# Output stage of a gated cross-attention and memory kernel: the stores move from ScalarE's queue to GpSimd's

## The reference

```
x = x + tanh(g_xattn) * softmax(Q K^T / sqrt(2048)) ctx      Q from layernorm(x), K from ctx
h = layernorm(x)
x = x + tanh(g_ffn) * (h + gate * aux),   aux = top-8 of 512 slots, softmax, values, down (128) and up (2048)
```

## Time and profile before

| | |
|---|---|
| median of 3 runs | 1082.8 us (1082.01 to 1083.5) |
| the profiled execution | 1081.9 us, of which the span of its instructions is 1079.8 us |
| granted TensorE clock, mean | 0.986 |
| PE busy | 1040.5 us (96%) |
| DVE busy | 784.7 us (73%) |
| ACT busy | 561.7 us (52%) |
| POOL busy | 183.2 us (17%) |
| output stage | from about 913 us to the end of the span |
| DMA | 218.93 MB over the span, mean 203 GB/s |

### The profile page before, as it was taken

The page is one execution under the profiler, slowest core; times in us unless marked ns, Lnnn a source line. Parts: engine busy times, 40 slices in busy tenths (PEclk is TensorE's granted clock), DMA queues, the critical chain, the costliest instruction groups (busy, mean ns, idle before and its releaser), DMA issues. The chain is left out here.

```text
span 1079.8 us, 19306 instructions
## 1 busy us (share of the span) xinstructions
PE 1040.5 (96%) x6778; PEld 995.8 (92%) x6778; DVE 784.7 (73%) x1845; ACT 561.7 (52%) x881; POOL 183.2 (17%) x351
## 2 busy tenths in 40 slices
PE   6999999998989999999999999999999994999997
PEld 6999999998989999999999999999999993888885
DVE  4889645466668787777777687877778766788785
ACT  3644777546435545454545445454545444555643
POOL 0007001000002222223231222222232321000000
PEclk9999999999999999999999999999999996999999
DMA  8556658598269965743445735257434418999999
GB/s 237 158 157 197 265 185 329 195 309 274 71 186 246 232 154 137 192 119 114 113 120 147 182 81 152 78 134 195 119 114 113 120 39 265 376 391 407 406 422 380
DMA packets 109615, 218.93 MB, mean 203 GB/s; under 512 B 48388, under 2 KB 64804, under 8 KB 95528
## 3 DMA queue, kind: packets, MB, share of 16 engines
q1 hardware_dynamic: 99784, 180.68, 55.0%
q10 hardware_dynamic: 9216, 33.56, 8.0%
q0 software_dynamic: 576, 4.19, 0.9%
HBM read 174.10 MB, written 54.79 MB: 212 GB/s over the span
## 5 line engine op out<-in xcount | busy, mean ns | idle before, releaser
L56 PE MATMUL tk_bank<-b_weights,k_turned 128*128 128x384 f32 (+2 forms) x1088 | 359.8, 331 | 3.4 <-DVE k_turned L1428 1.6
L58 PE MATMUL tk_bank<-b_weights,k_turned 128*128 128x384 f32 (+2 forms) x1088 | 350.9, 322 | 0.0
L57 PE MATMUL tk_bank<-b_weights,k_turned 128*128 128x384 f32 (+2 forms) x1088 | 350.7, 322 | 0.0
L56 PEld LDWEIGHTS tk_bank<-b_weights,k_turned 128*128 128x128 f32 x1088 | 205.2, 189 | 6.8 <-issue 2.6
L57 PEld LDWEIGHTS tk_bank<-b_weights,k_turned 128*128 128x128 f32 x1088 | 205.4, 189 | 1.2
L58 PEld LDWEIGHTS tk_bank<-b_weights,k_turned 128*128 128x128 f32 x1088 | 205.0, 188 | 0.0
L1419 DVE STREAM_TRANSPOSE tk_bank<-k_rows 128x512 f32<-128x512 f32 x128 | 133.7, 1068 | 5.9 <-DMA k_rows<-in_x_dram 5.5
L1231 ACT ACTIVATE k_turned<-tk_bank 128x512 fp32r<-128x512 f32 x128 | 73.7, 595 | 80.9 <-DVE tk_bank L1419 74.0
L1428 DVE TENSOR_TENSOR k_turned<-tk_bank,k_turned 128x512 fp32r<-128x512 f32 x128 | 82.7, 685 | 8.0 <-ACT k_turned L1231 6.8
L1794 DVE TENSOR_TENSOR late_x<-late_x,ob_out 128x512 f32<-128x512 f32 x96 | 65.7, 687 | 24.5 <-PE ob_out L58 23.0
L56 PE MATMUL tk_bank<-k_turned,a_T 128*128 128x256 f32 x256 | 75.1, 293 | 1.2 <-DVE a_T L343 0.7
(11 more groups left out here) (230 smaller groups left out, 2220.2 us busy)
## 6 DMA issues: line engine op xcount, KB each, us to landing
k_rows<-in_x_dram SPq DMA_DIRECT2D x40, 1024.0 KB, 4.9
k_rows<-in_x_dram SPq DMA_DIRECT2D x128, 256.0 KB, 5.1
late_x<-in_x_dram SPq DMA_DIRECT2D x24, 1024.0 KB, 8.6
out_dram<-late_x ACTq DMA_DIRECT2D x48, 512.0 KB, 14.5
k_rows<-in_Wq_dram SPq DMA_DIRECT2D x16, 1024.0 KB, 5.2
k_rows<-in_Wk_dram SPq DMA_DIRECT2D x9, 1024.0 KB, 4.8
out_dram<-k_rows ACTq DMA_DIRECT2D x16, 512.0 KB, 11.3
k_rows<-in_Wk_dram SPq DMA_DIRECT2D x28, 256.0 KB, 5.2
```

The lines of the kernel that those rows point to most:

```text
L56: pe.matmul(out, lh, rh, start=start, stop=False, skip_group_check=skip)
L57: pe.matmul(out, lh, rl, start=False, stop=False, skip_group_check=skip)
L58: return pe.matmul(out, ll, rh, start=False, stop=stop, skip_group_check=skip)
```

## The change

The function `store` leaves ACT's stream and goes, with the same waits, the same transfers and the same semaphores, into a stream for POOL of its own. POOL's program for the block is now: first and second store of tile 0, of tile 1, and so on to tile 31, then the wait for all eight slots. In ACT's stream hi, affine and context_high remain, in the same order.

```diff
-            def store(t, s, half):
-                cols = slice(half * D // 2, (half + 1) * D // 2)
-                act.wait_ge(S["added"], 4 * t + 2 * half + 2)
-                act.dma_start(xout[t][:, cols], x[s][:, cols]).then_inc(stored[s], 16)
...
                 if t + 1 < TILES:
                     hi(t + 1, (t + 1) % 2)
-                store(t, t % RING, 0)
                 if t + 1 < TILES:
                     affine(t + 1, (t + 1) % RING)
-                store(t, t % RING, 1)
                 b, k = divmod(t, PER_BATCH)
                 if k == 4 and b + 1 < BATCH:
                     context_high(act, keep, keep["ctx_hi"], b + 1)
+
+        @block.gpsimd
+        def _(pool):
+            def store(t, s, half):
+                cols = slice(half * D // 2, (half + 1) * D // 2)
+                pool.wait_ge(S["added"], 4 * t + 2 * half + 2)
+                pool.dma_start(xout[t][:, cols], x[s][:, cols]).then_inc(stored[s], 16)
+
+            for t in range(TILES):
+                store(t, t % RING, 0)
+                store(t, t % RING, 1)
             for s in range(RING):
-                act.wait_ge(stored[s], 32 * (TILES // RING))
+                pool.wait_ge(stored[s], 32 * (TILES // RING))
```

## The result

The changed kernel takes 1087.84 us, median of 8 runs (1085.91 to 1089.22), beside 1083.15 us, median of 8, for the kernel before (1079.75 to 1085.31). The ratio is 1.0046 with a 95% interval of 1.0032 to 1.0060, so it is slower by 3.5 to 6.5 us: under half a per cent, and clear of the noise. The forecast was 1083.2, no change.

The account below looks back on a forecast made before the run. PE with its last store and the DMA bytes were taken to end the stage almost together. Profiled 1081.9 plus 0.4 us for the last store, other terms 0, gave 1082.3, carried to the median as 1083.2 us; range 1081.8 to 1088.0.

Parts of the forecast that it names:

- a lower DMA rate: Rival: POOL's queue drives the DMA engines 2.1% slower, +1.2 to +2.9 us, 1084.0 to 1085.7 us; chance 0.15.
- a held-up DVE: Rival: each issue on POOL holds DVE up for its whole 0.538 us, +5.9 us, 1089 us; chance 0.08.
- What bounds the kernel: End of the stage: PE with its last store and the sheer number of DMA bytes finish almost together; cushion 2.8 us.
- Part 1, ACT's issues: ACT's queue loses 64 store issues, 21.6 us of otherwise idle time; gain nothing.
- The 0.8 us: ACT's next affine starts some 0.8 us earlier, from 0.5 us waiting plus the 0.34 us issue; nobody waits for it.
- Parts 2 and 3, when stores leave and what an issue costs: Stores leave POOL after their second addition as before; issues cost 531 to 768 ns against 338 on ACT, hidden by backlog.
- Part 4, the last store: Tail of the kernel: last store lands in 4.8 to 6.0 us against 5.3; with the hand-over of waits, +0.4 us.
- Part 5, the rate of the DMA engines: Whole stage: POOL's and ACT's queues read as equally fast within 2%, so nothing entered; one per cent less is 1.6 us.
- few transfers in flight: Rival: POOL's queue holds only two stores at a time, +36 us, 1119 us; chance 0.06.
- POOL's descriptors starved: Stores starved by DVE's three scalings a tile, 775 ns: only shifts stores in the backlog, 0; within the 0.08 DVE–POOL rival.

## Why the prediction was wrong

The forecast was no change, and the kernel is slower by 4.7 us. That 1087.84 us still lies inside the stated range, up to 1088.0, is luck: the upper part of the range was kept for a lower DMA rate and a held-up DVE, and the loss came from neither.

- *What bounds the kernel*: right. PE is the chain up to the last addition, the DMA engines are full, and the rows after agree.
- *Part 1, ACT's issues*: right in what it is worth, and wrong in one reading. The 0.8 us counts the store's issue twice: hi ends at 1066.62 and the affine starts at 1067.13, and the issue, 1066.74 to 1067.08, lies inside these 0.51 us. The affine starts 0.6 us earlier against the last addition. Nobody gained by it; ratio 1.0000 with 56 stores moved.
- *Parts 2 and 3, when stores leave and what an issue costs*: right in kind. 0.53 us each; the last store leaves 0.29 us after its addition, 0.26 later than from ACT.
- *Part 4, the last store*: this is where the prediction failed, in the sentence that the sum "also holds the hand-over of eight waits from ACT to POOL, for which the trace shows no cost". The waits cost nothing measurable (ratio 1.0000 with them alone on POOL). But behind the waits stands the block's drain, and I costed none, on any engine. On ACT it was 14 ns, on POOL after 64 DMAs it is 5286 ns: +5.3 us against my +0.2 at most, and it goes by the number of DMAs. The landing of the last store, bounded at 4.8 to 6.0 us, took 6.5, 6.7, 5.1 and 6.6 on POOL, but on ACT it also went up to 7.0: the scatter is larger than the term, and the bounds, worked out from three landings of POOL's DMAs in the first stage, were too narrow.
- *Part 5, the rate of the DMA engines*: 398 and 397 GB/s against 401 and 404 in the two pairs of profiles, but 402 with all stores on POOL and only the waits on ACT, and 402 and 405 in the two other kernels with ACT's stores. The two groups overlap, so a lower rate, of 1% or so, is not shown; PE never waits for a load in the changed kernel. With 56 stores on POOL it was 399 GB/s at a ratio of 1.0000. Entering nothing was right.
- *The rivals*: none was the mechanism. A hold-up of DVE did not occur (its sum rose by 0.96 us over 139), nor few transfers in flight (landing median 13.7 us at a full share). The Trainium skill (SBUF — State Buffer, SBUF: two separate sides) has POOL's descriptors starved while VectorE runs an operation in a fast mode that holds the port pair they share. DVE's three short scalings a tile, the operations that could do so here, left no mark: an issue on POOL at 1049.46, beside a scaling that starts at 1049.41, took 0.53 us like the others, and the median landing is no longer than from ACT.

The trace of before had the row that should have warned me, in the first stage, where POOL's four DMAs are followed by a drain:

```profile
L1383 POOLq DRAIN  x1: 8571/8571/8571, 178.0 to 178.0; - x1
```

It would have bounded the missing term at 0 to 8.6 us. It would not have given the size: that drain waits for a landing at about 186.4 (issued about 178.1, 8.3 us) and ends some 0.2 us later, which says nothing of 64 DMAs. The number came only from the runs.

## What to carry to other kernels

## What the runs showed of the hardware

POOL's drain, entered after all its DMAs have landed, by the number of DMAs that it has issued in the stretch since its drain before:

| DMAs | carrying | drain, us | 0.060 + 0.0817 x number |
|---|---|---|---|
| 0 | - | 0.041 | 0.06 |
| 1 | 512 KB | 0.141 | 0.14 |
| 8 | 8 x 512 KB | 0.707 | 0.71 |
| 32 | 32 x 1 MB | 2.672 | 2.67 |
| 64 | 64 x 512 KB | 5.286 | 5.29 |
| 128 | 128 x 256 KB | 10.512 | 10.52 |

The formula was worked out from the rows with 1, 8 and 64 DMAs; those with 32 and 128 came after it. So it is about 82 ns for each DMA, whatever it carries. The drains of SP and ACT show nothing of the kind: 14 ns on ACT after 64 landed stores, 158 ns on ACT with the last of 64 in flight. Entered with DMAs in flight, POOL's drain ends 2.2 to 2.7 us after the last of POOL's landings (56, 56 and 64 DMAs: 1074.2 against 1072.0, 1081.6 against 1079.3, 1082.5 against 1079.8). That is about half of what it takes alone, 5.3 us after 64 DMAs and by the formula 4.6 after 56. What POOL does in this time, and why only half of it fits beside the landing, no record shows; that stays open.
